# Expert weights split one stage early, expert outputs added by the gather engine's queue, and a Hadamard rotation moved from activations to weights

## The reference, cut to what matters

```python
x = x + cross_attention(layernorm(x), ctx)     # 16 heads of 128, Wq/Wk/Wv/Wo, rms norm of q and k
x = x + hadamard_ffn(layernorm(x))             # below
x = x + selective_scan(ctx, layernorm(x))      # 16 states, d_inner 512
x = x + moe(layernorm(x))                      # below

def hadamard_ffn(input):                       # 512 -> 2048 -> 512
    x = fwht(input * SU_ug) / SCALE            # Walsh-Hadamard transform over the 512 features
    x_up   = x @ W_up.T   * (Wscale_ug[:INTER] * SCALE)
    x_gate = x @ W_gate.T * (Wscale_ug[INTER:] * SCALE)
    x = fwht(silu(x_gate) * x_up * SU_dp) / SCALE
    return x @ W_down.T * (Wscale_dp * SCALE)

def moe(xt):                                   # 2048 tokens, 16 experts of 512 -> 256 -> 512, top 2
    probs = softmax(xt @ Wr.T + bias); topk_val, topk_idx = top_k(probs, 2)
    w = topk_val / (sum(topk_val) + EPS)
    y = (silu(xt @ Wg[e]) * (xt @ Wu[e])) @ Wd[e]        # for the two experts e of a token
    return sum over the two of w * y  +  (silu(xt @ sWg) * (xt @ sWu)) @ sWd
```

## Time and profile before

| | before |
|---|---|
| median of three runs | 2648.81 us |
| span of the profiled execution | 2643.4 us |
| PE busy | 2284.0 us (86%) |
| DVE busy | 1797.4 us (68%) |
| ACT busy | 1279.1 us (48%) |
| POOL busy | 1356.7 us (51%) |
| moved by DMA | 363.49 MB, mean 138 GB/s |

### The profile page before, as it was taken

How to read it: one execution, slowest core, us unless ns; L and a number is a source line. 1 busy time by engine, 2 the same in 40 slices (tenths; PEclk the granted TensorE clock), 3 DMA queues, 4 the chain that set the end, 5 groups by cost and what they waited for, 6 DMA issues and landing times. The chain is left out here.

```text
span 2643.4 us, 35123 instructions
## 1 busy us (share of the span) xinstructions
PE 2284.0 (86%) x10784; PEld 1760.5 (67%) x10785; DVE 1797.4 (68%) x3239; ACT 1279.1 (48%) x2275; POOL 1356.7 (51%) x1104
## 2 busy tenths in 40 slices
PE   3699999999999999999693899998998869578980
PEld 2688888888887888887442666665665547456770
DVE  6466777768677777876683998898988966312323
ACT  2344454444454444544383866757766632223430
POOL 0232333323333333333293988989979941488324
PEclk8799999999999999999886999999999988789995
DMA  7513232122322232211348565555565321665317
GB/s 286 216 53 113 88 112 79 58 109 89 113 78 79 88 113 89 87 64 39 131 166 265 168 208 204 175 185 187 196 183 183 123 84 48 215 219 173 117 52 266
DMA packets 136761, 363.49 MB, mean 138 GB/s; under 512 B 21264, under 2 KB 58768, under 8 KB 118416
## 3 DMA queue, kind: packets, MB, share of 16 engines
q1 hardware_dynamic: 123504, 328.30, 36.1%
q0 software_dynamic: 6320, 20.71, 2.4%
q10 hardware_dynamic: 6768, 12.32, 1.2%
HBM read 289.99 MB, written 71.30 MB: 137 GB/s over the span
## 5 line engine op out<-in xcount | busy, mean ns | idle before, releaser
L641 POOL TENSOR_SCALAR att_probs<-att_probs,att_recip 128x512 f32<-128x512 f32 x256 | 181.8, 713 | 562.6 <-DVE att_recip L708 562.6
L1819 POOL TENSOR_TENSOR mix_drive<-mix_du,mix_rows 128x512 f32<-128x512 f32 x256 | 326.6, 1282 | 48.8 <-DVE mix_state L1891 15.9
L565 ACT ACTIVATE att_probs<-att_s,att_bias,att_rq 128x512 f32<-128x512 f32 x256 | 200.6, 784 | 288.3 <-DVE att_bias L704 288.1
L1891 DVE TENSOR_TENSOR_SCAN mix_state<-mix_state,mix_drive 128x512 f32<-128x512 f32 x256 | 312.9, 1222 | 30.8 <-POOL mix_drive L1819 17.3
L1671 ACT ACTIVATE mix_state<-mix_delta,mix_a 128x512 f32<-128x512 f32 x256 | 175.8, 690 | 227.8 <-DVE mix_drive L1902 187.4
L1804 POOL TENSOR_TENSOR mix_y<-mix_y,mix_drive 128x512 f32<-128x512 f32 x180 | 230.6, 1281 | 46.0 <-DVE mix_drive L1902 45.8
L1580 PE MATMUL mix_down<-mix_wd,mix_hT 128*128 128x512 f32 x512 | 232.0, 596 | 8.8 <-DVE residual_x L1922 8.8
L703 DVE TENSOR_REDUCE att_nmax<-att_s 128x1 f32<-128x512 f32 x256 | 175.1, 684 | 71.4 <-PE att_s L101 64.6
L744 DVE TENSOR_TENSOR att_pT<-att_pt,att_pT 128x512 fp32r<-128x512 f32 x256 | 170.1, 686 | 66.0 <-ACT att_pT L571 61.9
L571 ACT CAST att_pT<-att_pt 128x512 fp32r<-128x512 f32 x256 | 144.2, 593 | 133.4 <-PE att_pt L422 129.2
L99 PE MATMUL att_w<-att_w_qkv,att_cx 128*128 128x256 f32 x512 | 158.7, 310 | 35.2 <-DVE att_w_qkv L690 26.5
(11 more groups left out here) (354 smaller groups left out, 6703.7 us busy)
## 6 DMA issues: line engine op xcount, KB each, us to landing
att_xn<-normT SPq DMA_DIRECT2D x32, 2048.0 KB, 8.7
mix_gu<-guT SPq DMA_DIRECT2D x64, 1024.0 KB, 8.2
mix_rows<-bc_d SPq DMA_DIRECT2D x128, 256.0 KB, 4.8
guT<-att_ffnT SPq DMA_DIRECT2D x32, 512.0 KB, 5.7
mix_wd<-wdT SPq DMA_DIRECT2D x16, 1024.0 KB, 7.9
slots<-exp_y ACTq DMA_DIRECT2D x47, 256.0 KB
normT<-nrm_outT SPq DMA_DIRECT2D x4, 2048.0 KB, 9.1
exp_raw<-in_L_ffn_Wg SPq DMA_DIRECT2D x16, 512.0 KB, 5.1
```

The source lines that it names most:

```text
L565: act.activation(probs[:, n, :], ps_s[n % 2][:, :], ACT.Exp, bias=bias[:, n:n + 1], scale=rq[:, n:n + 1], accum_out=sums[:, n:n + 1]).then ...
L641: pool.tensor_scalar(probs[:, n, :], probs[:, n, :], recip[:, n:n + 1], 1.0, ALU.mult, ALU.mult).then_inc(s_pn, 1)
L1819: pool.tensor_tensor(drive[q % RING][:, :], du[i % DUS][:, :], rows[g % ROWS][:, 0, :], ALU.mult).then_inc(s_drive, 1)
L1891: dve.tensor_tensor_scan(h[:, :], h[:, :], drive[q % RING][:, :], 0.0, ALU.mult, ALU.add).then_inc(s_scan, 1)
```

## The change

**Attention.** All loops are written out, none is left in hardware. ctx is kept in two buffers instead of four and reloaded (1 MB) in each iteration. Two pieces of work are new in each iteration:

- The FFN weight tile is rotated before it is split. POOL does two levels of the transform as additions and subtractions of halves (`butterflies`), PE transposes, ACT and DVE split (`ffn_hi`, `ffn_lo`), PE multiplies by the 128x128 Hadamard matrix (`rotate_ffn`), ACT copies out.
- Half an expert's weights (128x1536 per half, 0.79 MB) is loaded, split by POOL (`split_expert`) and stored split to DRAM (`split_w`, 1.57 MB).

```diff
+                def rotate_ffn(i):
+                    pe.wait_ge(s_tlo, i + 1)
+                    pe.wait_ge(s_ptlo, 8 * i + TB + 2)
+                    pe.matmul(ps_pt[1][:, :, :], had_sb[:, :], fT[:, 0, :, :], start=True, stop=False)
+                    pe.matmul(ps_pt[1][:, :, :], had_sb[:, :], fT[:, 1, :, :], start=False, stop=True).then_inc(s_fr, 1)
...
+                def ffn_lo(i):
+                    dve.wait_ge(s_thi, i + 1)
+                    dve.tensor_tensor(fT[:, 1, :, :], ps_pt[0][:, :, :], fT[:, 0, :, :].bitcast(F32),
+                                      ALU.subtract).then_inc(s_tlo, 1)
...
+                def butterflies(i):
+                    pool.wait_ge(s_fraw, 16 * (i + 1))
...
+                        for two, op in ((0, ALU.add), (1, ALU.subtract)):
+                            pool.tensor_tensor(d_v[:, :, two, :], s_v[:, :, 0, :], s_v[:, :, 1, :], op).then_inc(s_bf, 1)
...
+                def split_expert(i):
+                    pool.wait_ge(s_ein, 80 * (i // 2) + (32, 80)[i % 2])
+                    raw_w = ew[:, 1, :].bitcast(F32)
+                    pool.tensor_scalar(ew[:, 0, :], raw_w, 1.0, 1.0, ALU.mult, ALU.mult).then_inc(s_ehi, 1)
+                    pool.wait_ge(s_ehi, i + 1)
+                    pool.tensor_tensor(ew[:, 1, :], raw_w, ew[:, 0, :].bitcast(F32), ALU.subtract).then_inc(s_elo, 1)
```

```diff
-                def rotate(b, o):
...
-                        mm = pe.matmul(spare[o % 2][:, :], hs[:, g, k, :], normT[:, k, :], start=(k == 0), stop=(k == KD - 1))
...
+                        if j == 7:
                             turn(b + 1, 0)
                             turn(b + 1, 1)
```

```diff
+                def load(e):
+                    sp.dma_start(w[:, e % WRING, :, :].bitcast(F32), split_w[e]).then_inc(s_load[e % WRING], 16)
...
+                    end = sp.value_load(plan.ends[0:1, e - WRING:e - WRING + 1], min_val=1, max_val=TILES)
+                    wait_apart(sp, s_y, end, s_pace)
+                    load(e)
...
+                sp.wait_ge(s_add, 16 * TILES)
+                sp.dma_start(out, mixed[0:B * S, :]).then_inc(s_out, 16)
...
+                def add(k):
+                    pool.wait_ge(s_yout, k + 1)
+                    if k:
+                        pool.wait_ge(s_add, 16 * k)
+                    pool.indirect_dma_start(mixed, bass.IndirectOffsetOnAxis(plan.target[:, k:k + 1], 0),
+                                            yout[k % YS][:, :], None, compute_op=ALU.add).then_inc(s_add, 16)
...
+                    if k >= YS:
+                        act.wait_ge(s_add, 16 * (k - YS + 1))
+                    act.activation(yout[k % YS][:, :], ps_y[k % 2][:, :], ACT.Copy,
+                                   scale=weight[:, k:k + 1]).then_inc(s_yout, 1)
```

More of the change, by code:

```diff
@@ L359, in iteration @@
                         load_wo(hp + 1)
[L360 removed]
+                    if hp < PAIRS - 1 or b < B - 2:
                         sp.wait_ge(s_q, 2 * i + 4)
@@ L681, in iteration @@
                         norm_q(j)
+                    split_expert(i)
+                    if not last:
+                        butterflies(j)
                 pairs(pool, iteration)
@@ L781, in _, with iteration @@
                 row_max(own, 0, 1)
-                base = own.n
-                per_pair = B * (8 + 1) + 3
-                def iteration(own, hp, b, last):
+                def iteration(hp, b, last):
                     i = hp * B + b
                     j = i + 1
-                    more = not isinstance(hp, int)
+                    more = hp < PAIRS - 1
                     row_recip(i, 0)
@@ L839, in iteration @@
                         add_y(i, b, t)
[L841 to L853 removed]
+                pairs(dve, iteration)
 STATES = 16
@@ L1128, in _ @@
                             if b:
-                                rotate(b - 1)
+                                turn(b - 1)
                         if t == 1:
@@ L1141, in _ @@
                         turn_down(s + 3)
-                rotate(KD - 1)
+                turn(KD - 1)
             @block.scalar
@@ L1233, in _ @@
                 down_hi(1)
-                norm_out(3)
+                for t in range(TB):
+                    norm(t)
                 down_out(1)
@@ new lines, in add @@
+                def add(k):
[4 more added lines that the diff above has]
+                                            yout[k % YS][:, :], None, compute_op=ALU.add).then_inc(s_add, 16)
+                for k in range(AHEAD):
+                    gather(k)
+                for k in range(TILES):
+                    if k + AHEAD < TILES:
+                        gather(k + AHEAD)
+                    add(k)
@@ new lines, in expert, with gate_up @@
+                def expert(k):
+                    return pe.value_load(plan.expert[0:1, k:k + 1], min_val=0, max_val=EXPERTS - 1)
+                def gate_up(k, now, s):
+                    pe.wait_ge(s_w, now + 1)
+                    pe.wait_ge(s_xlo, k + 1)
+                    if k >= 2:
+                        pe.wait_ge(s_h, k - 1)
+                    for c in range(KD):
+                        at = c * 2 * INNER
+                        mm = split_product(pe, ps_g[k % 2][:, :, :], (xT[k % 2][:, 0, c, :], xT[k % 2][:, 1, c, :]),
+                                           (part(s, 0, at, 2 * INNER), part(s, 1, at, 2 * INNER)), c == 0, c == KD - 1)
+                    mm.then_inc(s_g, 1)
@@ new lines, in down @@
+                def down(k, s):
+                    pe.wait_ge(s_hlo, k + 1)
+                    if k >= 2:
+                        pe.wait_ge(s_yout, k - 1)
+                    for c in range(IC):
+                        at = N_IN + c * DIM
+                        mm = split_product(pe, ps_y[k % 2][:, :], (hT[k % 2][:, 0, c, :], hT[k % 2][:, 1, c, :]),
+                                           (part(s, 0, at, DIM), part(s, 1, at, DIM)), c == 0, c == IC - 1)
+                    mm.then_inc(s_y, 1)
@@ new lines, in _ @@
+                pe.wait_ge(s_id, 16)
+                turn_x(0)
+                for k in range(TILES + 1):
+                    if k >= 1:
+                        before = slot
+                        turn_h(k - 1)
+                    if k + 1 < TILES:
+                        turn_x(k + 1)
+                    if k < TILES:
+                        now = expert(k)
+                        slot = now % WRING
+                        gate_up(k, now, slot)
+                    if k >= 1:
+                        down(k - 1, before)
```

714 lines of the change are left out of this document (292 added, 422 removed).

## The result

The changed kernel takes 2743.05 us (median of four runs, 2739.7 to 2748.29) against 2649.02 of the kernel before: 1.036 times as long, 95% interval 1.034 to 1.038. It was forecast at 2641 us, a little faster. Its profiled span is 2737.9 us, 94.5 more than before. That execution took 2739.7 us, 1.8 more than its span, and was the fastest of the four; so of the 5.4 us that the forecast adds to a span, most is the distance from one execution to the median.

The account below looks back on a forecast made before the run. PE alone was taken to set attention's pace (1082.0 of 1108 us busy). Attention +65, prep -7, mix -5, router +1 and experts -62 summed to -8 us: span 2635, time 2641 us, range 2591 to 2698.

Parts of the forecast that it names:

- the pace of the adds: Experts: each add waits for the previous landing, 6.0 us for 36 tiles, 4.9 for 10; stage 311 us, -62 us.
- the adds are the bound: Rival, experts: each scatter lands after 7 us beside the loads; stage gains only 5 us, time 2698; chance 0.20.
- The loops: Attention: writing out six turns of the hardware loop saves 24 us, 4 us each (8.9 to 27).
- The rotation: Attention: PE waits 1.2 us for ffn_lo plus 0.45 for two products, in 31 iterations: +51 us (14 to 80).
- POOL beside DVE: Attention: POOL's new work holds up DVE, +35 us at split_w in seven third iterations, +3 at the small L704 operations.
- the two cases: Attention, third iterations: o_lo 3.7 us late if only subtractions are blocked, 6.2 us if casts are too.
- the term at 43: Attention: the delay at split_w if DVE's casts are blocked by POOL as well, 43 us instead of 35.
- Mix: Mix stage: removing 96 rotation rows, 57 us of PE at most, gives back -5 us (0 to -25).
- Prep's -7: Prep stage: 16 rotate products go, at most 19 us of busy PE, about a third of it gained: -7 us.
- a sum of -8: Whole kernel: all stage terms together make it 8 us faster, span 2635, time 2641 us.
- terms of +65 and -62: Attention in sum 65 us longer (-10 to +110); experts and combine 62 us shorter.
- the upper bound of the experts' stage, -5: Experts: with 7 us per tile the stage takes 368 us, only 5 us less than before.

Follow-up runs that it names:

- third experiment: Changed kernel with the addition left out of the experts' indirect scatter, which only writes the rows: span 2677.4 us, experts to the end 324.0 us.
- the fourth: Changed kernel without the weight loads of the 12 experts behind the first four: span 2660.0 us, experts 311.8 us.
- fifth experiment: Changed kernel with the later 12 experts' loads in six pieces of 0.52 MB, at most two in flight: span 2700.3 us, experts 360.3 us.
- the first: Changed kernel with POOL's expert-weight split begun only after DVE's split in the third iteration of seven pairs: median 2707.27 us, 1.024 times the kernel before.
- the eighth experiment: Changed kernel with POOL's split behind DVE's, plus rq as scalar of the small DVE operation: attention ends at 1304.4 us, span 2697.3 us.

## Why the prediction was wrong

**The step that failed** is the pace of the adds: "So p = 6.0 for 36 tiles and 4.9 for 10, mean 5.76". It was 7.33, and with a first result after 29 us and not 22 the stage took 387.9 us and not 311. That is 77 of the 102 us between 2641 and 2743, 72 of them by the pace. It failed in two ways. A step alone was taken as 4.9, PE's pace, with no price for the add itself; it was 5.5, of which the addition is 2.0 (third experiment), and once the buffers were full PE was no longer the bound. A step beside a load was taken as an average share of 303 GB/s, 5.2 to 6 us; it was 11.7, because an add that was issued behind a load of 3.15 MB landed only behind it (its landings in the trace, and the fourth and fifth experiment). Why it has to, the runs do not show: both go to the same DRAM, from different queues. Both are in the term that carried the rival "the adds are the bound", with a mean of 7 and a chance of 0.20. Its mechanism was the right one; the rows of before could not price it, since none of their landings was of a transfer that adds, and none stood beside a single transfer of 3 MB.

The rule of the Trainium skill that I weighed there (page DMA: Bandwidth & Descriptors, section "Anatomy of one DMA — SWDGE (gpsimd) path"), 2.0 us plus the bytes, would have given 2.6 us for an add (an estimate from the page's figures). The runs show 5.5 alone and 11.7 beside a load. For a plain scatter of the same rows, 3.5 us from one to the next, it is nearer.

**The loops** were sized right: 24 us forecast, 24.7 measured to attention's end, 22.6 of them within attention.

**The rotation** came out at 50.9 us against 51, but not by my working. The wait for `ffn_lo` is 0.57 and not 1.2 us: the change itself moved `split_ffn` out of `scale_k`'s way, which no row of before could show. The other terms are 14.7 for the products and 17.4 for the waits, 32 of the 51; 8 us are clock, which the sum had nothing for, and 11 are not assigned. That the sum agrees is luck.

**POOL beside DVE** was forecast at +35 and +3 and is 44 us by the first and the eighth experiment (29.4 + 14.7). The mechanism was right. `o_lo` was late by 4.3 us, between the 3.7 and the 6.2 of the two cases (the four lengths given for the second add up to 6.35). The casts are held up too: 0.89 and 1.21 instead of 0.69 us, each begun when the POOL operation had 0.3 to 0.7 us left and not at its beginning. That agrees with the rule of the Trainium skill, page SBUF — State Buffer, section "SBUF: two separate sides", by which I had the term at 43. What I left out is what a wait does to PE's clock: 2.4 us behind six of the seven, 1.4 behind the other.

With 3 or 4 us for the rest of the split, the parts give -24.7 + 50.9 + 44.1 + 4 = 74.3 of the 74.6 us measured. Each is the difference of single executions that can be some us off, so the agreement to 0.3 is chance.

**Mix** gave back nothing of its 29 us. PE's waits in mix, after the change and then before it:

```profile
PE mix_up L99 <- DVE mix_hT L1909: 71.9, 55, 4.3
PE mix_gate L99 <- DMA mix_skip<-in_L_xattn_D: 45.4, 1, 45.4
```

```profile
PE mix_gate L99 <- DMA mix_skip<-in_L_xattn_D: 37.6, 1, 37.6
PE mix_up L99 <- DVE mix_hT L1916: 34.2, 27, 3.4
```

The waits for `mix_hT` of DVE are 37.7 us longer, as much as the work removed and more. The wait for a small table (`mix_skip`) is 8 us longer, but most of that lies ahead of the stage, in which the first product stands after 25.1 us instead of 23.5. DVE, for its part, waited 8.6 us less for PE's down products (16.9 instead of 25.5, the term that the -5 was taken from) and 12.9 us more for ACT's `mix_state` (25.8 instead of 12.9). So the stage did give back what the forecast counted on, and lost more at another wait; why ACT is later there, and with it the +4.9, stays open. That DVE and POOL are as full as PE was named in the prediction; the -5 should have been 0 at best. Prep's -7 was hidden in the same way: 12 us of PE's work less, 0.5 us of time.

The way the working stood, a sum of -8 out of terms of +65 and -62 could not carry a forecast of "faster" at all. The range ended 45 us short because the upper bound of the experts' stage, -5, was not a bound but the far end of the same guess.

## What to carry to other kernels

A chain of transfers in which each waits for the landing of the one before costs its full latency for each link, and a link issued behind a long transfer cost that transfer's length here: price a link with the transfer beside it, not with the mean rate. Results in plain stores, several in flight, took the chain away; loads in pieces shortened the links but made the weights late. When GpSimd is given work in a gap, look at what VectorE does in that gap: two-input operations from SBUF are held up for a whole GpSimd operation; a small one whose second operand is passed as a scalar was not. Work taken off an engine that is not the bound of its stage can be worth nothing (12 us of PE's in prep gave 0.5, 29 in mix gave none), and work put where that engine is the bound is paid in full, with the waits that it brings and the clock lost behind the long ones on top.

## What the runs showed of the hardware

- An indirect DMA of 128 rows of 2 KB that adds into DRAM is 5.2 to 6.5 us from one issue to the next when each waits for its landing, 3.5 without the addition, and 10.9 to 12.7 when it is issued during a load of 3.15 MB, which itself takes 10.9 to 13.4. In twelve cases it landed 0.2 to 0.7 us behind such a load; issued 2.8 to 3.9 us ahead of the load, it landed after 4.8 to 5.1, six times. Its issue takes 1.59 us of POOL against 0.95 to 0.99 for a gather.
- A turn of the hardware loop in attention costs 3.8 us (22.6 over six).
- After a wait of 4.3 us TensorE's products followed each other at 0.43 us, the lower of its two levels (granted clock 0.50), for 12 products, and then at 0.24.
- A VectorE operation of 128x1 with two inputs took up to 2.74 us beside a GpSimd operation; with one input and a scalar none of 256 took over 0.22. Larger ones with one input were held up (128x128 beside `split_ffn`: 366 against 321 ns in the mean, the casts of 128x1024: 0.89 and 1.21 against 0.69 us).
